# Recurrent layer of an eight-stage model on one core: half of the input loads issued by GpSimd, and the cell state written twice

## The reference

```
x_proj = x W_ih^T + b_ih + b_hh
step:  i, f, g, o = split(xp + h W_hh^T)
       c = sigmoid(f) * c + sigmoid(i) * tanh(g)
       h = sigmoid(o) * tanh(c)
logits = h W_lin^T + b_lin ;  w = argmax(logits) * h
out = 2 h + (cumsum(w) - w) * fw_att + (sum(w) - cumsum(w)) * bw_att
```

## Time and profile before

| | us |
|---|---|
| median of three runs | 4351.86 |
| lowest and highest | 4345.56, 4361.19 |
| the profiled execution's own time | 4350.92 |
| its span | 4349.1 |
| PE busy | 3997.5 (92%) |
| DVE busy | 3562.1 (82%) |
| ACT busy | 3025.4 (70%) |
| POOL busy | 1176.2 (27%) |
| first and last H of the recurrent part | 2918.2, 4274.1 |

### The profile page before, as it was taken

The page is one execution under the profiler, slowest core; times in us unless marked ns, Lnnn a source line. Parts: engine busy times, 40 slices in busy tenths (PEclk is TensorE's granted clock), DMA queues, the critical chain, the costliest instruction groups (busy, mean ns, idle before and its releaser), DMA issues. The chain is left out here.

```text
span 4349.1 us, 150269 instructions
## 1 busy us (share of the span) xinstructions
PE 3997.5 (92%) x58273; PEld 2799.1 (64%) x58273; DVE 3562.1 (82%) x10111; ACT 3025.4 (70%) x7562; POOL 1176.2 (27%) x1025
## 2 busy tenths in 40 slices
PE   8999999996999999999998999988888888888882
PEld 5666666653666656666665777867777776777772
DVE  7999999996898898898887888866777777777776
ACT  7999999995888888888885776754444444444441
POOL 4777777762222222222222111100000000000000
PEclk9999999998999999999999999999999999999996
DMA  2222222211000000000002443421111111121115
GB/s 68 81 84 68 79 63 74 78 54 37 25 25 30 21 30 30 21 30 30 21 25 67 137 137 119 137 81 29 45 39 45 38 44 42 40 46 36 45 38 170
DMA packets 328467, 251.45 MB, mean 58 GB/s; under 512 B 174284, under 2 KB 292428, under 8 KB 325708
## 3 DMA queue, kind: packets, MB, share of 16 engines
q1 hardware_dynamic: 326220, 233.39, 18.3%
q10 hardware_dynamic: 1536, 8.39, 0.6%
HBM read 157.26 MB, written 67.11 MB: 52 GB/s over the span
## 5 line engine op out<-in xcount | busy, mean ns | idle before, releaser
L1615 ACT ACTIVATE ssm_EX<-ssm_Z_psum,ssm_tok 128x256 f32<-128x256 f32 (+1 forms) x1024 | 371.9, 423 | 156.0 <-PE ssm_Z_psum L1446 86.2
L2710 ACT ACTIVATE lstm_TF<-lstm_FO_psum 128x64 f32<-128x64 f32 x512 | 114.2, 223 | 467.7 <-PE lstm_FO_psum L2617 463.3
L2617 PE MATMUL lstm_FO_psum<-next_Whh,lstm_HT 128*32 128x64 f32 x8192 | 221.7, 226 | 183.2 <-DVE lstm_HT L2780 182.4
L647 ACT ACTIVATE g_PR<-g_S,g_nmax 128x512 f32<-128x512 f32 x512 | 368.5, 723 | 4.0 <-DVE g_nmax L784 4.0
L791 DVE COPY g_PT<-g_PT_psum 128x512 f32<-128x512 f32 x512 | 344.3, 683 | 26.1 <-PE g_PT_psum L514 21.6
L638 ACT ACTIVATE g_relu<-g_Z_psum,g_src 128x512 f32<-128x512 f32 x512 | 346.6, 683 | 21.1 <-PE g_Z_psum L507 21.0
L784 DVE CUSTOM_DVE_ANT_0 g_S<-g_Z_psum,g_relu 128x512 f32<-128x512 f32 x512 | 345.3, 684 | 10.4 <-ACT g_relu L638 8.9
L2936 POOL TENSOR_SCALAR lstm_rstd<-lstm_mv 128x4 f32<-128x4 f32 x32 | 7.3, 229 | 1245.9 <-DVE lstm_mv L2755 1245.9
L514 PEld LDWEIGHTS g_PT_psum<-kept_ident,g_PR 128*128 128x128 f32 x2048 | 242.4, 141 | 136.8 <-ACT g_PR L647 54.3
L2602 PE MATMUL lstm_FO_psum<-next_Wih,lstm_XT 128*32 128x128 f32 x8192 | 325.9, 276 | 1.1 <-ACT lstm_XT L2704 0.7
L2602 PE MATMUL lstm_IG_psum<-next_Wih,lstm_XT 128*32 128x128 f32 x8192 | 322.8, 274 | 0.1
(11 more groups left out here) (309 smaller groups left out, 10907.0 us busy)
## 6 DMA issues: line engine op xcount, KB each, us to landing
g_ADJ<-in_adj SPq DMA_DIRECT2D x64, 1024.0 KB, 7.0
x<-g_XO SPq DMA_DIRECT2D x64, 512.0 KB, 5.3
g_X<-in_x SPq DMA_DIRECT2D x32, 512.0 KB, 4.3
ssm_X<-x SPq DMA_DIRECT2D x32, 512.0 KB, 3.9
x<-ssm_OUT SPq DMA_DIRECT2D x32, 512.0 KB, 2.9
g_X<-x SPq DMA_DIRECT2D x32, 512.0 KB, 4.3
lstm_U<-x SPq DMA_DIRECT2D x128, 128.0 KB, 3.0
lstm_V<-lstm_U SPq DMA_DIRECT2D x128, 128.0 KB, 2.9
```

What stands on the lines that cost most here:

```text
L647: act.activation(PR[n % 4][:, :], S[n % 4][:, :], ACT.Exp, scale=-1.0, bias=nmax[:, n % 4:n % 4 + 1], accum_out=rsum[b.slot][:, t, HH * p ...
L1615: ins = act.activation(EX[h % NE][:, col:col + n], Zb[c][:, i * CHUNK:i * CHUNK + n], ACT.Exp, bias=tok[b.slot][:, i, c, h:h + 1])
L2617: ins = pe.matmul(FOb[t % 2][32 * j:32 * (j + 1), 0:HB], turned_state(c, t, kc), Whh[:, kc, j, HB:2 * HB], start=False, stop=(kc == KC - 1 ...
```

## The change

Two things change in the recurrent part. The loads of a chunk are split: SP issues those of the raw tiles 0 and 2, POOL those of the tiles 1 and 3, and each group has its own semaphore. The `bn_stats` of tile 0 waits for SP's 16 loads, that of tile 1 for POOL's 16. POOL issues its loads ahead of the scales of the same chunk, behind the same wait as SP.

And the new cell is computed by two equal instructions: the first writes it into columns 128 to 191 of the bank IG of that step, where ACT's tanh reads it; the second writes C in SBUF as before, and KP of the next step waits for that one. The wait of the tanh is on the first.

```diff
-        names = ("w setup_v raw_in st mv rstd shift0 shift xn xt_pe xt gf g go tf tg to keep inp c2 tc h ht lgp lg flag "
+        names = ("w setup_v raw_in raw_in_g st mv rstd shift0 shift xn xt_pe xt gf g go tf tg to keep inp c2 c2s tc h ht lgp lg flag "
@@ SP
             def load(c):
                 c.wait(sp, s["xn"], TILES, 0)
-                for k in range(TILES):
+                for k in range(0, TILES, 2):
                     for b in range(BT):
                         sp.dma_start(raw[S * b:S * (b + 1), k, :], xv[c.index()][BT * k + b]
                                      ).then_inc(s["raw_in"], 16)
@@ ACT
                 c.wait(act, s["c2"], S, t + 1)
-                act.activation(tc[:, :], C[:, :], ACT.Tanh, scale=0.5).then_inc(s["tc"], 1)
+                act.activation(tc[:, :], IGb[t % 2][:, 2 * HB:3 * HB], ACT.Tanh, scale=0.5).then_inc(s["tc"], 1)
@@ DVE
                 if k == 0:
-                    c.wait(v, s["raw_in"], 16 * P // S * TILES, 0)
+                    c.wait(v, s["raw_in"], 8 * P // S * TILES, 0)
                     c.wait(v, s["xn"], TILES, 0)
+                if k == 1:
+                    c.wait(v, s["raw_in_g"], 8 * P // S * TILES, 0)
@@ DVE
-                c.wait(v, s["c2"], S, t)
+                c.wait(v, s["c2s"], S, t)
@@ DVE
+                v.scalar_tensor_tensor(out=IGb[t % 2][:, 2 * HB:3 * HB], in0=KP[:, :], scalar=0.5, in1=IN[:, :],
+                                       op0=ALU.mult, op1=ALU.add).then_inc(s["c2"], 1)
                 v.scalar_tensor_tensor(out=C[:, :], in0=KP[:, :], scalar=0.5, in1=IN[:, :], op0=ALU.mult, op1=ALU.add
-                                       ).then_inc(s["c2"], 1)
+                                       ).then_inc(s["c2s"], 1)
@@ POOL
+            def load(c):
+                c.wait(g, s["xn"], TILES, 0)
+                for k in range(1, TILES, 2):
+                    for b in range(BT):
+                        g.dma_start(raw[S * b:S * (b + 1), k, :], xv[c.index()][BT * k + b]).then_inc(s["raw_in_g"], 16)
+
             def body(c):
                 if c.reg is not None or c.off < CH - 1:
+                    load(c + 1)
                     scales(c + 1)
```

## The result

| | before | after |
|---|---|---|
| median, lowest and highest of five runs (us) | 4351.81 (4345.56 to 4361.19) | 4328.06 (4324.87 to 4330.16) |
| the profiled execution's own time, its span | 4350.92, 4349.1 | 4329.99, 4328.2 |
| first to last H | 1355.9 | 1334.0 |
| DVE's waits for a raw tile | 29.5 us, 23 times | none |

The ratio is 0.9944, with a 95% interval of 0.9930 to 0.9959: faster by 24 us, or 0.6%. It was forecast as 4316.0 (4298 to 4346); the measured median lies in that range, at the upper end of the band of 4300 to 4328 that had got a chance of 0.52. So the sign and the mechanism were right, and the gain of 35 us came out as 21 us in the profiled execution and 24 between the medians. What follows is about the 12 to 14 us that are missing.

The account below looks back on a forecast made before the run. Bound by a chain of waits round one loop per recurrent step, plus DVE's waits for loads. From 4350.9 us, loads take off 19.1 and the cell 15.8, giving 4316.0, range 4298 to 4346.

Parts of the forecast that it names:

- the band of 4300 to 4328: Whole kernel: the time band in us around the forecast of 4316.0, given a chance of 0.52.
- Loads: Start of each chunk's statistics: splitting loads between SP and POOL removes DVE's waits, 19.1 us gone of 21.7.
- the 1.1 us left for chunk 1: POOL's loads in chunk 1: expected 1.1 us late once, at 1.04 us a load, so kept as remaining loss.
- Cell: Between C and H: tanh reading the cell from PSUM saves 33 ns in 480 of 511 intervals, 15.8 us.
- a pair of rows that only read: DVE at 128x512: 676 ns with one input in PSUM or both in SBUF, so 0 taken for writing too.
- +65 for DVE and -42 for ACT: Cell and tanh by the Trainium skill's access times: +23 ns a step, about 12 us slower in all.
- PSUM gives nothing: Rival: writing the cell to PSUM costs DVE 25 to 66 ns longer; 4331.8 to 4347.6 us, chance 0.22.
- POOL slow: Rival at step 4's wait for POOL's loads: above 1.35 us a load costs time, 4395 at 1.5; chance 0.13.
- Loads no sooner: Rival: DMA engines, not SP, set the loads' pace, waits stay; 4335 us, chance 0.06 including late by tenths.
- DVE late for H: Rival: PSUM write also delays DVE's next instruction by 60 ns or more beyond the spare; 19 us, 4335, chance 0.07.
- the 0.06 us: DVE's spare time before H, with the SBUF copy hidden behind ACT's tanh, in ten steps of 16.

Follow-up runs that it names:

- e3_paced: The changed kernel, with SP waiting for H of step 4 before moving V and H of step 8 before fetching U: 4321.85 us, ratio 0.9939 to before.
- e9_loads_paced: Split loads with the single cell in SBUF, plus the two SP waits of e3_paced: 4330.65 us, ratio 0.9953 to the kernel before.
- e2_cell: The changed kernel with the second cell kept but all 32 loads of a chunk given back to SP: 4340.97 us, ratio 0.9986 to before.
- e4_third: The changed kernel with a third, unused copy of the cell in SBUF behind the second: 4344.54 us, ratio 0.9993 to before.
- e8: e3_paced with the load of U moved from behind H of step 8 to behind H of step 10: 4324.16 us, ratio 0.9938 to before.
- e1_loads: The changed kernel with the split loads kept and the second cell taken back: 4333.74 us, ratio 0.9966 to the kernel before.

## Why the prediction was right, and by what it missed

**Loads: forecast 19.1, got 11.7 us in the profiled execution** (15.0 and 16.5 in the two others). The waits went as worked out, and with the moves elsewhere the loads are worth 19.5 (e3_paced) and 19.6 (e9_loads_paced), the term of the sum. POOL's price was mis-sized: 0.49 us where 1.04 was taken from the earlier trace rows and SP's 0.61 was called the lower end. It was below that end. That cost nothing but the 1.1 us left for chunk 1, which did not occur. What failed is the half sentence "on SP the moves of V and U come 10 us earlier, and nobody waits for them sooner". True, nobody waits for their data. But they moved from about steps 3 to 7 onto steps 0 to 4, where PE's fetches came late behind them and PE has no slack at the logits of step 4. Steps 3 and 4 took 4.5 to 7.9 us back in the three executions. What the movement costs differs between executions of one program (losses of 10.3, 7.0 and 5.5), so single medians show it poorly.

**Cell: forecast 15.8, got 10.2 us.** The step saves 22 ns (2.581 to 2.559), not 33. ACT's 33 are all there. Against them, the write to PSUM takes DVE 7 ns more where I had taken 0 from a pair of rows that only read; by the medians of their starts tc begins 268 ns after the cell instead of 259, and H 256 after tc instead of 288. And step 13 gains nothing either (2.60 in both), so 450 steps and not 480 count: 450 x 22 ns = 9.9. The access times of the Trainium skill ("Perfetto Trace Analysis", Optimizing Scalar/DVE Operations), which I had weighed as +65 for DVE and -42 for ACT, have both signs right and the first size wrong here: the write cost 7 to 9 ns, and ACT gained 33. Where they and the rows differ, the rows decide: the step is shorter by 22 ns, not longer by 23.

The two shortfalls are of like size, 7.4 and 5.6 us, and with the 0.9 at the ends they are the 14 us that the profiled execution misses; no error hid another.

**The rivals.** PSUM gives nothing: refuted by e2_cell, whose clean chunk is 0.33 shorter. POOL slow: refuted by 0.49. Loads no sooner: refuted, no wait is left. DVE late for H: e4_third showed that the 0.06 us was right; with two cells it is not used up. The rival that happened in part was not in the list: a transfer that nobody waits for, in the way of instruction fetches.

**What is not shown.** That the moves of U and V and the stops belong together is shown in both directions, by e3 and e8, and by the fetches of fourteen traces. How the packets delay the fetch is not. In chunk 8 of after it started 0.6 us after the last of them, in chunk 3 of e8 in their midst. Why e1_loads lost 3.0 us at steps 3 and 4 and the changed kernel 4.5 to 7.9 stays open too: there is one profiled execution of e1, and the spread of the changed kernel alone is 3.4. That PE waits for the fetched instructions is inferred from the narrow 2.2 to 2.5 us between the fetch and the end of a stop; the profile names no wait.

## What to carry to other kernels

Where a change frees an issuing queue, write down every transfer that stands behind in it, and where each will lie then: beside the question who waits for its data stands the question what runs through the DMA engines at that time, instruction fetches of a busy engine among them, and whether that engine has slack there. Move such transfers with a wait to steps with slack; here two waits gave 3 to 5 us between medians. In a loop whose engines wait for one another in turn, the memory of each operand between ACT and DVE is worth testing in both directions: one more cell on DVE, hidden behind the tanh, bought 22 ns a step, and the tanh's output in PSUM another 18.

## What the runs showed of the hardware

- A DMA of 16 rows of 1 KB issued by POOL takes 0.48 to 0.49 us of POOL, in rows of 16 and of 32; SP needs 0.50 to 0.70 for the same by the rows of 16 loads of all runs.
- ACT's tanh of 128x64 float32 takes 256 ns from SBUF to SBUF, 223 from PSUM to SBUF, 208 from PSUM to PSUM. DVE's 128x64 instruction with two SBUF inputs takes 226 ns with its output in SBUF (219 for the second of two in a row) and 233 with it in PSUM; H with one input in PSUM takes 221 instead of 226.
- Where PE stopped without a wait in the changed kernel, it resumed 2.2 to 2.5 us after the start of a 16 KB instruction fetch: 12 stops, 6.8 us from start to start in one execution. Over fourteen traces 120 of 900 fetches with data packets in flight came late, and 17 of 3664 without.
- POOL starts its loads 3.1 us late before its 129th load, its 257th and each 128 further, in twelve of twelve traces in which it issues any, with nothing named by the profile; why is not known.
